# Cross-attention with layer norm: the first value step waits for one batch of V, and some softmax row sums move from VectorE to ScalarE's accumulators

## What is computed

```python
qs = (q @ wq).reshape(Bq, Lq, H, HD).transpose(0, 2, 1, 3)
ks_ = (k @ wk).reshape(Bq, Lk, H, HD).transpose(0, 2, 1, 3)
vs = (v @ wv).reshape(Bq, Lk, H, HD).transpose(0, 2, 1, 3)
scores = jnp.einsum('bhqd,bhkd->bhqk', qs, ks_) / jnp.sqrt(jnp.float32(HD))
scores = jnp.where(mask[:, None, :, :], -jnp.inf, scores)
attn_w = jax.nn.softmax(scores, axis=-1)
attn = jnp.einsum('bhqk,bhkd->bhqd', attn_w, vs)
out = attn.transpose(0, 2, 1, 3).reshape(Bq, Lq, H * HD) @ wo + q
mu = jnp.mean(out, axis=-1, keepdims=True)
var = jnp.mean((out - mu) ** 2, axis=-1, keepdims=True)
return (out - mu) / jnp.sqrt(var + EPS) * gamma + beta
```

## Time and profile before

| | |
|---|---|
| time, median of 3 runs (lowest to highest) | 643.67 us (642.51 to 645.41) |
| the profiled execution's own time | 644.07 us |
| its span, first to last instruction | 642.0 us |
| PE busy | 615.1 us, 96% |
| DVE busy | 529.2 us, 82% |
| ACT busy | 509.3 us, 79% |
| POOL busy | 494.9 us, 77% |
| mean granted clock of PE | 0.993 of full speed |

### The profile page before, as it was taken

The page is one execution under the profiler, slowest core; times in us unless marked ns, Lnnn a source line. Parts: engine busy times, 40 slices in busy tenths (PEclk is TensorE's granted clock), DMA queues, the critical chain, the costliest instruction groups (busy, mean ns, idle before and its releaser), DMA issues.

```text
span 642.0 us, 12451 instructions
## 1 busy us (share of the span) xinstructions
PE 615.1 (96%) x3816; PEld 486.0 (76%) x3816; DVE 529.2 (82%) x1009; ACT 509.3 (79%) x1558; POOL 494.9 (77%) x639
## 2 busy tenths in 40 slices
PE   7998799999999999999999999999999999998975
PEld 5766587887878788787878788787878878786754
DVE  5867678888889788888889988888879988888797
ACT  4877688888878888888888888887888888787550
POOL 6466459797978979797978979797996979577674
PEclk9999999999999999999999999999999999999899
DMA  8451112221231322222231322232122212412003
GB/s 293 142 183 31 57 34 83 100 88 62 100 109 66 102 79 101 65 91 92 98 112 50 100 71 94 83 99 100 67 93 90 89 45 66 165 61 72 18 17 132
DMA packets 34785, 57.75 MB, mean 90 GB/s; under 512 B 6816, under 2 KB 7840, under 8 KB 34720
## 3 DMA queue, kind: packets, MB, share of 16 engines
q1 hardware_dynamic: 34720, 56.96, 26.9%
HBM read 39.53 MB, written 16.78 MB: 88 GB/s over the span
## 4 chain that ended last, share of the span: by engine, by line
PE 84%; DVE 10%; ACT 3%; issue 1%; POOL 0%; DMA 0%; POOLq 0%; SPq 0%; DVEq 0%; ACTq 0%
PE bank L381 25%; PE bank L306 24%; PE bank L329 15%; PE bank L339 8%; PE bank L360 4%; PE bank L365 2%; ACT pr L484 2%; PE bank L343 2%; DVE pr L619 2%; DVE sm L632 2%; PE bank L286 2%; DVE nm L625 2%; PE bank L299 2%; DVE st L656 1%; DVE pf L598 1%
## 5 line engine op out<-in xcount | busy, mean ns | idle before, releaser
L484 ACT ACTIVATE pr<-pr,nm 128x77 f32<-128x77 f32 x1024 | 270.2, 347 | 67.1 <-DVE nm L625 65.0
L778 POOL TENSOR_TENSOR pn<-pr,rec 128x512 f32<-128x512 f32 x128 | 135.2, 1056 | 96.6 <-DVE rec L634 95.0
L619 DVE SCALAR_TENSOR_TENSOR pr<-msk,bank 128x308 f32<-128x308 uint8 x256 | 109.4, 468 | 43.2 <-PE bank L329 43.2
L632 DVE TENSOR_REDUCE sm<-pr 128x8 f32<-128x616 f32 x128 | 99.8, 780 | 12.1 <-ACT pr L484 10.7
L625 DVE TENSOR_REDUCE nm<-pr 128x8 f32<-128x616 f32 x128 | 101.8, 795 | 4.4
L381 PE MATMUL bank<-woh,ah 128*128 128x512 f32 x256 | 101.8, 398 | 2.8 <-DVE al L641 1.9
L306 PE MATMUL bank<-xh,wqh 128*128 128x512 f32 x256 | 103.0, 402 | 1.3 <-DVE ql L607 1.3
L453 ACT ACTIVATE ptr<-bank 128x512 f32<-128x512 f32 (+1 forms) x256 | 95.3, 426 | 9.2 <-PE bank L339 9.2
L381 PE MATMUL bank<-woh,al 128*128 128x512 f32 x256 | 101.7, 397 | 0.0
L381 PE MATMUL bank<-wol,ah 128*128 128x512 f32 x256 | 101.4, 396 | 0.0
L306 PE MATMUL bank<-xh,wql 128*128 128x512 f32 x256 | 100.6, 393 | 0.0
(11 more groups left out here) (67 smaller groups left out, 1062.2 us busy)
## 6 DMA issues: line engine op xcount, KB each, us to landing
xraw<-xT SPq DMA_DIRECT2D x59, 256.0 KB, 3.0
xres<-x SPq DMA_DIRECT2D x58, 256.0 KB, 2.7
out<-y SPq DMA_DIRECT2D x56, 256.0 KB, 2.0
wk_sb<-wk SPq DMA_DIRECT2D x4, 256.0 KB, 4.1
wq_raw<-wq SPq DMA_DIRECT2D x4, 256.0 KB, 6.2
wv_sb<-wv SPq DMA_DIRECT2D x1, 1024.0 KB, 8.9
wo_raw<-xT SPq DMA_DIRECT2D x4, 256.0 KB, 8.8
wo_raw<-wo SPq DMA_DIRECT2D x1, 1024.0 KB, 6.2
```

The costliest lines, as they stand in the source:

```text
L484: last = nc.scalar.activation(s, s, ACT.Exp, bias=nm[:, t % 2, h:h + 1], scale=1.0)
L619: nc.vector.scalar_tensor_tensor(out=pr[:, 4 * g:4 * g + 4, :], in0=msk[:, b % 2, t % TB, :].unsqueeze(1).broadcast_to([P, 4, LK]), scalar ...
L632: nc.vector.tensor_reduce(sm[:, t % 2, hs], pr[:, hs, :], AX.X, ALU.add).then_inc(v_sum, 1)
L778: nc.gpsimd.tensor_tensor(pn[:, half, 0:4, :].rearrange("p s (e k) -> p (s e) k", e=2), pr[:, hs, 0:KM], rec[:, t % 2, hs].unsqueeze(2).br ...
```

## The change

It does three things.

1. The semaphore `d_vm` becomes two. The first value step waits for batch 0's 10 DMAs alone (`d_vm[0]`); the 32 DMAs of batches 1 to 3 (`d_vm[1]`) are waited for by `project_o(0)`, in iteration 6.
2. `SUMS = (6, T - 4)`: in iterations 6 to 59 the row sums stay on VectorE. In iterations 0 to 5 and 60 to 63, 20 halves in all, each of the eight ACTIVATEs of a half also writes the sum of its results, as `accum_out`, to its column of `sm`, and VectorE only takes the reciprocals, as soon as the half's exponentials are done.
3. `ah` and `al` now take the place of `wo_raw` and of `ctx_sb` (which is made as wide as they are), and `z` and `y` that of `vs`. So `keep_a(0)` on ScalarE gets a wait for GpSimd's split of the output weights (`g_wo`).

```diff
+SUMS = (6, T - 4)
...
-            ctx_sb = early("ctx_sb", [P, KT, NB * LK])
+            ctx_sb = early("ctx_sb", [P, KT, D])[:, :, 0:NB * LK]
             vs = early("vs", [P, 3, 4, 2, 2, HD])
         qh0 = sb("qh0", [P, NG, D], f32r)
         qh1 = sb("qh1", [P, NG, D], f32r)
+        ah = sb("ah", [P, NG, D], f32r)
+        al = sb("al", [P, NG, D], f32r)
         z = sb("z", [P, 2, D])
         y = sb("y", [P, YS, D])
-        ah = sb("ah", [P, NG, D], f32r)
-        al = sb("al", [P, NG, D], f32r)
...
-        d_vm = sem("d_vm")
+        d_vm = [sem(f"d_vm{i}") for i in range(2)]
...
-                                         vs[at:at + n, i, :, e].rearrange("p s h d -> p s (h d)")).then_inc(d_vm, 16)
+                                         vs[at:at + n, i, :, e].rearrange("p s h d -> p s (h d)")).then_inc(d_vm[b > 0], 16)
...
-                                             vs[at + KM - lo:at + LK - lo, i, s, e]).then_inc(d_vm, 16)
+                                             vs[at + KM - lo:at + LK - lo, i, s, e]).then_inc(d_vm[b > 0], 16)
...
                 if e == 0:
-                    pe.wait_ge(d_vm, 42 * 16)
+                    pe.wait_ge(d_vm[0], 10 * 16)
                     pe.wait_ge(a_v, 3)
...
                 if t == 0:
                     pe.wait_ge(g_wo, 2 * KT)
+                    pe.wait_ge(d_vm[1], 32 * 16)
...
                 for h in range(HH * half, HH * half + HH):
                     s = pr[:, h, :]
-                    last = nc.scalar.activation(s, s, ACT.Exp, bias=nm[:, t % 2, h:h + 1], scale=1.0)
+                    if SUMS[0] <= t < SUMS[1]:
+                        last = nc.scalar.activation(s, s, ACT.Exp, bias=nm[:, t % 2, h:h + 1], scale=1.0)
+                    else:
+                        last = nc.scalar.activation(s, s, ACT.Exp, bias=nm[:, t % 2, h:h + 1], scale=1.0,
+                                                    accum_out=sm[:, t % 2, h:h + 1])
...
             def keep_a(e):
                 t, n = STEPS[e]
+                if e == 0:
+                    act.wait_ge(g_wo, 2 * KT)
...
                 dve.wait_ge(a_exp, n)
-                nc.vector.tensor_reduce(sm[:, t % 2, hs], pr[:, hs, :], AX.X, ALU.add).then_inc(v_sum, 1)
-                dve.wait_ge(v_sum, n)
+                if SUMS[0] <= t < SUMS[1]:
+                    nc.vector.tensor_reduce(sm[:, t % 2, hs], pr[:, hs, :], AX.X, ALU.add).then_inc(v_sum, 1)
+                    dve.wait_ge(v_sum, n - 2 * SUMS[0])
                 nc.vector.reciprocal(rec[:, t % 2, hs], sm[:, t % 2, hs]).then_inc(v_rec, 1)
```

## The result

The changed kernel takes 641.3 us (median of 16 runs, 640.34 to 642.14); the kernel before, measured beside it, 644.86 us (16 runs, 641.73 to 646.51). The ratio is 0.9948, with a 95% interval of 0.9935 to 0.996: about 3.4 us faster, a small gain that the interval keeps clear of no change. The profiled execution took 641.83 us, with a span of 640.0.

A forecast was written before the change was run, and what follows sets the result against it. The tensor engine bounds the kernel, busy 615 of 642 us, with open time only at start and end. Start -0.1 and last tiles -0.2, -0.2, -0.7 make -1.2 us, so 642.5 us; own range 640 to 646.5, 8-in-10 range 635.0 to 652.0.

The forecast's parts named there:

- a = 0.07: Upper end of the rival that the accumulator is nearly free (chance 0.38): some -3.7 us, 640.0 us.
- The price a: Time added to each ScalarE ACTIVATE that also accumulates; taken as 0.095 us, the lost overlap between instructions.
- a pass of its own: Rival: reading the accumulator on ScalarE is a separate pass, 0.17 us each; +7.1 us, 650.8 us; chance 0.24.
- 0.116 us an operand: ScalarE price per [128,1] operand, from an ACTIVATE of 816 ns with two against 584 without, at 128x512.
- Part 1: First value step's wait for V: without it PE could start at 68.9, not 71.94; worth 3.0 us by itself.
- the 3.03 us gap at 71.94: PE's gap before the first value step, blamed on V's placement; its removal was to bring nothing through the clock.
- Part 2: Sums of iterations 0 to 5 moved off VectorE: 2.7 us gained in all, 64a added on ScalarE.
- -6.3 + 64a: Shift in us of the first value step's second half, 3.6 of it from the wait; -0.2 at a = 0.095.
- the chain: Eight halves of exponentials, (0,0) to (4,1), 64 instructions, ending with ScalarE's copy of (3,1); three sums leave it.
- Part 3: Gaps of the last tiles, in three places: -0.2, -0.2 and -0.7 us at a = 0.095.
- the clock as a rival: Shorter gaps in the last tiles keep PE's clock up: up to 1.9 and 1.4 us more; no separate chance.
- What would show it: Signs: eight exponentials take 2.8 us, the value step's gap goes, 0.5 to 1 us may stand between matmuls 16 and 17.

The follow-up runs named there:

- kernel with fillers: Kernel before plus 16 matmuls nobody reads, eight in the 1.95 us gap and eight in the 2.07 us gap: ratio 0.9969 to the kernel before.
- split into halves: Kernel with split wait and ScalarE sums in the last four tiles, plus start sums in five second halves (0.9891) or six first halves (0.9929); ratios to kernel before.

## Why the prediction was right, and where its steps were off

It gave 642.5 us, 1.2 below a median of 643.67; measured were 641.3, 3.4 below by the ratio. The mechanism was right: the split wait gains some 3 us, the dearer exponentials of the start give it back, and what remains comes from the last tiles. The size is near the fast end of the forecast's own range (640 to 646.5), and about what it gave for a = 0.07, 3.7 us below, though a is 0.09. Two things in it were luck: the price came out nearly right for a wrong reason, and the time stayed inside the range though the clock was left out of the sum.

- **The price a** was taken as 0.095 and is 0.09. The reason was wrong, so the close value is luck: no overlap is lost, the ACTIVATE keeps its length. An instruction of its own follows, which lasts 189 ns and adds 0.09, with the same 0.094 us hidden beneath its neighbour as every other. The rival "a pass of its own" had the mechanism right, and priced it by the shortest copy, which has 128 columns, not one. The 93 ns for a [128,1] pointer operand that the Trainium skill gives (page "ScalarE: Activation LUTs", section "What ACT_TABLE_LOAD costs") came near the price, for something else: the trace shows no longer ACTIVATE. And the prediction's 0.116 us an operand compared unlike rows. The ACTIVATE with two such operands reads SBUF, while the 584 ns are for a copy out of PSUM; the copy of the same size that reads SBUF lasts 627 ns in the kernel before, so an operand costs about (816 - 627)/2 = 95 ns. The two instructions differ in function and output type, so this is an estimate; it agrees with those 93 ns, and the prediction's remark that the trace's price is the higher one doesn't hold:

```profile
L453 ACT ACTIVATE xh<-xraw 128x512 fp32r<-128x512 f32 x59 | 37.0, 627 | 0.9 <-DMA xraw<-xT 0.8
```

- **Part 1** was said to be worth 3.0 us by itself. Measured alone, the value step starts 3.3 us earlier and the ratio gives 4.2 (2.9 to 5.5). Whether the rest of the 4.2 is clock isn't shown. But "the 3.03 us gap at 71.94 did not lower the clock at all, so its removal brings nothing of this kind" is seen in one execution only. In the profiled execution of the kernel with fillers, whose start is that of before, this step comes behind 3.38 us of idle time and is slower (1.95 us before for the same 32 matmuls), so the kernel before may lose clock here in some of its executions. The timeline and a stretch of PE in that run:

```profile
72.70 2.56 PE L360 MATMUL bank<-ptr,vm 64*32 64x512 f32 x32 [3.38 <-issue]
```
```profile
72.00:78.00 6.00, 5.30 (x53) 0.72 0.43 133
```

- **Part 2**, -6.3 + 64a: at a = 0.09 the copy of (3,1) should be ready at 69.35 - 2.7 + 5.8 = 72.4; it was at 72.7, with the first exponential 0.26 us sooner, so some 0.6 us later than the chain gives. The start of the change against before was given as -0.1 us; the trace has +0.3 at the first value step. The split into halves (-0.3 and +1.3, where the chain gives -0.4 and +1.9) bears out which of them count, with the first halves somewhat cheaper than given.
- **Part 3**, the last tiles, was given as -1.1 us (-0.2, -0.2 and -0.7), and this is the term that was too small. In the order of the work it was nearly right: between the two runs with the split wait, with and without the last tiles' sums, from the start of tile 56's value step, the third part of the output projection comes 0.35 us sooner (predicted 0.2), tile 59's projection another 0.14 (0.2), the last value step another 0.38 (0.7), 0.9 in all. The ratios give 2.6. The clock is the likely rest: mean granted 0.9933 without and 0.9970 with them, which is 2.4 us of 638 by estimate and so more than enough. Behind the start of the last value step the two profiles differ by another 1.2 us (636.9 - 618.16 = 18.7 and 635.0 - 617.47 = 17.5), where the former is at 0.81 and 0.77 of full clock. The fillers show that the clock can be raised in these gaps, in the kernel before; they weren't put into the run with the wait alone, so for the 2.6 us this share is argued and not measured by itself. I had the clock as a rival with up to 3.3 us, but the forecast took none of it; it should have been a term of the sum.
- **What would show it**: a row of eight exponentials was to take 2.8 us, and seven steps of 0.342 and the last 0.44 make 2.8. The gap before the value step is gone, as said. The gap between its 16th and 17th matmul is not there, since PE, at 0.76 of full clock from 65 to 72 us, came as late as ScalarE's copy.

## What to carry to other kernels

Before a sum is moved into another engine's instructions, write down for each place which engine's end is waited for. An exchange of 0.83 us on one engine for 0.72 on another is worth nothing where both stand in one chain, and costs most of its price where only the second does. A wait that ends last by 3 us can be taken away and show no gain, if the same change makes the next one last; timing each part alone (here in three kernels that differ from the changed one in a line) shows that a better kernel lay inside the change. And near the end of a kernel, where the tensor engine has gaps of 1 to 2 us, more of a gain may be the clock's than the order's: look at the clock of many runs, not of one profile.

## What was not expected of the hardware

- An ACTIVATE with `accum_out` is two instructions in the trace: 349 ns and 189 ns, one pair each 0.342 us where the plain one takes 0.253.
- With ScalarE summing in all iterations, most kinds of its instructions in the iterations lasted longer as a mean: 375 ns an exponential (349 with 160 of them accumulating), 216 the read (189), 611 the copy of 128x512 to `ptr` (584), 292 that of 128x128 (267). The copy to `ah` did not (583, 603 before), nor did those of the start, such as `kh` (419, 418 before). It is the recorded length that grows, and not the time used: the exponentials of a half still start 0.34 us apart. Why is open. The timeline of ACT in that run:

```profile
310.39 0.37 ACT L490 ACTIVATE pr<-pr,nm 128x77 f32<-128x77 f32 x1
310.64 0.21 ACT L490 ACTIVATION_READ_ACCUMULATOR pr<-pr,nm 128x1 f32 x1
310.73 0.36 ACT L490 ACTIVATE pr<-pr,nm 128x77 f32<-128x77 f32 x1
```

- Work that nobody reads, put into two gaps of PE, made the kernel before 2.0 us faster.
- Whether a gap lowers the clock differs between executions: behind 1.95 us it was 0.66 in one, behind 1.94 us at the same place full in another.
